# Attention: two heads share one product with V, 256 columns wide

## What is computed

```python
rep = N_HEADS // N_KV_HEADS          # 2: two heads share one K and V
kk = jnp.repeat(kk, rep, axis=1)
v = jnp.repeat(v, rep, axis=1)
att = jnp.einsum('shd,thd->hst', q, kk) / np.sqrt(HEAD_DIM)
causal = jnp.tril(jnp.ones((S, S), bool))
att = jnp.where(causal[None], att, jnp.finfo(att.dtype).min)
att = jax.nn.softmax(att, axis=-1)
attn_out = jnp.einsum('hst,thd->shd', att, v).reshape(S, N_HEADS * HEAD_DIM) @ wo
```

## Time and profile before

| | us |
|---|---|
| median of 3 runs | 2893.99 (2890.41 to 2895.43) |
| profiled execution, its time | 2896.59 |
| its span, first to last instruction | 2893.9 |
| attention loop of the first half | 1214.2 to 1260.6 |
| attention loop of the second half | 2416.6 to 2488.7 |

### The profile page before, as it was taken

The page is one execution under the profiler, slowest core; times in us unless marked ns, Lnnn a source line. Parts: engine busy times, 40 slices in busy tenths (PEclk is TensorE's granted clock), DMA queues, the critical chain, the costliest instruction groups (busy, mean ns, idle before and its releaser), DMA issues. The chain is left out here.

```text
span 2893.9 us, 33670 instructions
## 1 busy us (share of the span) xinstructions
PE 2383.4 (82%) x11480; PEld 1635.3 (57%) x11480; DVE 2070.8 (72%) x2611; ACT 1636.1 (57%) x3494; POOL 1621.8 (56%) x728
## 2 busy tenths in 40 slices
PE   8967887777788549896887888887886799999998
PEld 3345555555555318554666766665553485578863
DVE  5669999999999766425999999998997654210000
ACT  4578878888887343335887777886772313210000
POOL 0079999999999310005998998998993100000000
PEclk9979999999999759998999999998998899999999
DMA  7722242432522497742335325335225852244443
GB/s 275 264 77 81 81 144 73 137 108 66 167 66 62 165 372 285 255 174 100 99 95 179 102 92 179 101 93 178 92 76 206 306 181 66 84 142 153 153 153 102
DMA packets 236953, 418.47 MB, mean 145 GB/s; under 512 B 33904, under 2 KB 117872, under 8 KB 233968
## 3 DMA queue, kind: packets, MB, share of 16 engines
q1 hardware_dynamic: 223280, 360.22, 38.5%
q10 hardware_dynamic: 12160, 51.39, 4.5%
q0 software_dynamic: 1344, 4.72, 0.4%
HBM read 332.38 MB, written 83.89 MB: 144 GB/s over the span
## 5 line engine op out<-in xcount | busy, mean ns | idle before, releaser
L640 POOL TENSOR_TENSOR s_x<-s_du,k_bB 128x2048 f32<-128x2048 f32 (+1 forms) x256 | 881.5, 3456 | 30.9 <-issue 18.7
L716 PE MATMUL s_py<-k_ident,s_x 128*128 128x128 f32 x4096 | 562.1, 282 | 188.8 <-DVE s_x L1021 115.9
L716 PEld LDWEIGHTS s_py<-k_ident,s_x 128*128 128x128 f32 x4096 | 478.5, 145 | 410.2 <-DVE s_x L1021 192.7
L967 ACT ACTIVATE s_pA<-s_delta,k_negA 128x512 f32<-128x512 f32 x768 | 500.3, 681 | 184.4 <-DVE s_x L1021 179.3
L647 POOL TENSOR_TENSOR s_x<-s_hp,k_bC 128x1024 f32<-128x1024 f32 x192 | 452.4, 2371 | 28.0 <-DVE s_hp L1040 27.9
L1708 PE MATMUL l_p<-l_hT,l_ring 128*128 128x256 f32 x1792 | 389.6, 380 | 2.3 <-DVE l_hT L1899 1.3
L1021 DVE TENSOR_TENSOR s_x<-s_pA,k_bC 128x1024 f32<-128x1024 f32 x320 | 383.8, 1199 | 7.2 <-DMA k_bC<-scratch_xd 7.1
L1708 PEld LDWEIGHTS l_p<-l_hT,l_ring 128*128 128x128 f32 x1792 | 341.8, 191 | 50.0 <-issue 1.9
L867 ACT ACTIVATE s_xT<-s_duT,k_BT 128x128 f32<-128x128 f32 x1024 | 335.9, 387 | 0.1
L1040 DVE TENSOR_TENSOR_SCAN s_pA<-s_pA,s_x 128x512 f32<-128x512 f32 x256 | 302.5, 1215 | 39.9 <-ACT s_pA L967 39.3
L1040 DVE TENSOR_TENSOR_SCAN s_pA<-s_pA,s_carry,s_x 128x512 f32<-128x512 f32 x256 | 316.1, 1266 | 0.8 <-ACT s_pA L967 0.5
(11 more groups left out here) (212 smaller groups left out, 3669.1 us busy)
## 6 DMA issues: line engine op xcount, KB each, us to landing
k_bC<-scratch_xd SPq DMA_DIRECT2D x32, 1024.0 KB, 10.1
scratch_ug<-p_ug ACTq DMA_DIRECT2D x16, 1024.0 KB, 4.3
k_u<-scratch_ug SPq DMA_DIRECT2D x64, 256.0 KB, 3.5
k_bB<-scratch_xd SPq DMA_DIRECT2D x16, 1024.0 KB, 9.8
s_gy<-scratch_ug SPq DMA_DIRECT2D x64, 256.0 KB, 4.4
s_xt<-in_x SPq DMA_DIRECT2D x64, 256.0 KB, 4.7
scratch_x<-s_xt SPq DMA_DIRECT2D x64, 256.0 KB, 2.3
r_x<-scratch_x SPq DMA_DIRECT2D x32, 512.0 KB, 9.4
```

Of the source, the lines that this page charges most:

```text
L640: pool.tensor_tensor(out=x[:, 4 * g:4 * g + many], in0=du[:, s % 2:s % 2 + 1].broadcast_to([P, many, HALF]), in1=bB[:, 3 * g + g % 2:3 * g ...
L716: last = nc.tensor.matmul(py[:, a], x[:, n, a * P:(a + 1) * P], ident[:], is_transpose=True, start=False, stop=is_last and a == HALF // P - 1)
L967: nc.scalar.activation(out, delta[:, s % 2], ACT.Exp, scale=negA[:, s % NE, n:n + 1]).then_inc(dA_ready, 1)
```

## The change

The order of the combinations becomes: head = n // 4 * 2 + n % 2 and batch = n // 2 % 2. The two heads that share K and V come one after the other for the same batch, so the tile counts go 1, 1, 2, 2 in the first half and 3, 3, 4, 4 in the second. `probT` holds the pair side by side for each tile, twice its size before. PE makes one product with V for a pair, of 256 columns instead of 128, in every second step only (c - 3 odd), when the second of the pair is ready. ACT copies the outputs of both heads in one instruction of 256 columns. The other operations stay as they are, in the new order. ACT's copy to `probT` now writes blocks of 128 with a gap of 128 between them.

```diff
+    def head_of(n):
+        return n // (2 * SPAN) * 2 + n % 2
+    def batch_of(n):
+        return n // 2 % SPAN
+    def keys_of(n):
+        return (first + batch_of(n) + 1) * P
-    probT = sb("probT", [P, 2, KEYS * P])
+    probT = sb("probT", [P, 2, KEYS, 2, P])
...
-                if 0 <= c - 3 < COMBOS:
-                    n, kv = c - 3, (c - 3) // SPAN * NKV // NH
-                    tiles = first + n % SPAN + 1
+                if 0 <= c - 3 < COMBOS and (c - 3) % 2:
+                    n, m, kv = c - 3, (c - 3) // 2, head_of(c - 3) * NKV // NH
+                    tiles = keys_of(n) // P
                     pe.wait_ge(probT_ready, n + 1)
-                    at_least(pe, o_ready, n - 1)
+                    at_least(pe, o_ready, m - 1)
                     for b in range(tiles):
-                        last = nc.tensor.matmul(side[2 + n % 2][:, 0:P], v[:, b, kv * DH:(kv + 1) * DH],
-                                                probT[:, n % 2, b * P:(b + 1) * P], start=b == 0, stop=b == tiles - 1)
+                        last = nc.tensor.matmul(side[2 + m % 2][:, 0:2 * P], v[:, b, kv * DH:(kv + 1) * DH],
+                                                probT[:, m % 2, b].rearrange("p j s -> p (j s)"), start=b == 0, stop=b == tiles - 1)
...
                     act.wait_ge(p_turned, n + 1)
-                    at_least(act, o_done, n - 1)
-                    nc.scalar.activation(probT[:, n % 2, 0:end], side[n % 2][:, 0:end], ACT.Copy).then_inc(probT_ready, 1)
+                    at_least(act, o_done, m - 1)
+                    nc.scalar.activation(probT[:, m % 2, 0:tiles, n % 2], side[n % 2][:, 0:tiles * P].rearrange("p (b s) -> p b s", s=P),
+                                         ACT.Copy).then_inc(probT_ready, 1)
...
-                    nc.scalar.activation(o[:, head, a * P:(a + 1) * P], side[2 + n % 2][:, 0:P], ACT.Identity,
-                                         bias=cols[:, bv:bv + 1]).then_inc(o_ready, 1)
+                    nc.scalar.activation(o[:, head:head + 2, a * P:(a + 1) * P], side[2 + m % 2][:, 0:2 * P].rearrange("p (j s) -> p j s", s=P),
+                                         ACT.Identity, bias=cols[:, bv:bv + 1]).then_inc(o_ready, 1)
```

More of the change, by code:

```diff
@@ L1744, in _ @@
                 if c < COMBOS:
-                    n, head, a = c, c // SPAN, c % SPAN
-                    end = (first + a + 1) * P
+                    n, head, a, end = c, head_of(c), batch_of(c), keys_of(c)
                     at_least(pe, expd, n - 3)
@@ L1755, in _ @@
                     at_least(pe, probT_ready, n - 1)
-                    for b in range(first + n % SPAN + 1):
+                    for b in range(keys_of(n) // P):
                         last = nc.tensor.transpose(side[n % 2][:, b * P:(b + 1) * P], prob[:, n % 4, b * P:(b + 1) * P], ident[:])
                     last.then_inc(p_turned, 1)
-                if 0 <= c - 3 < COMBOS:
-                    n, kv = c - 3, (c - 3) // SPAN * NKV // NH
-                    tiles = first + n % SPAN + 1
+                if 0 <= c - 3 < COMBOS and (c - 3) % 2:
+                    n, m, kv = c - 3, (c - 3) // 2, head_of(c - 3) * NKV // NH
+                    tiles = keys_of(n) // P
                     pe.wait_ge(probT_ready, n + 1)
-                    at_least(pe, o_ready, n - 1)
+                    at_least(pe, o_ready, m - 1)
                     for b in range(tiles):
-                        last = nc.tensor.matmul(side[2 + n % 2][:, 0:P], v[:, b, kv * DH:(kv + 1) * DH],
-                                                probT[:, n % 2, b * P:(b + 1) * P], start=b == 0, stop=b == tiles - 1)
+                        last = nc.tensor.matmul(side[2 + m % 2][:, 0:2 * P], v[:, b, kv * DH:(kv + 1) * DH],
+                                                probT[:, m % 2, b].rearrange("p j s -> p (j s)"), start=b == 0, stop=b == tiles - 1)
                     last.then_inc(o_done, 1)
@@ L1770, in _ @@
             for k in range(NH):
-                pe.wait_ge(o_ready, SPAN * (k + 1))
+                pe.wait_ge(o_ready, SPAN * (k // 2 + 1))
                 rows_of(T_WO + k, o[:, k], acc, k == 0, k == NH - 1).then_inc(w_used, 1)
@@ L1842, in _ @@
                 if c < COMBOS:
-                    n, j, end = c, c % 4, (first + c % SPAN + 1) * P
+                    n, j, end = c, c % 4, keys_of(c)
                     act.wait_ge(biased, n + 1)
@@ L1848, in _ @@
                 if 0 <= c - 2 < COMBOS:
-                    n, end = c - 2, (first + c % SPAN + 1) * P
+                    n, m, tiles = c - 2, (c - 2) // 2, keys_of(c - 2) // P
                     act.wait_ge(p_turned, n + 1)
-                    at_least(act, o_done, n - 1)
-                    nc.scalar.activation(probT[:, n % 2, 0:end], side[n % 2][:, 0:end], ACT.Copy).then_inc(probT_ready, 1)
-                if 0 <= c - 3 < COMBOS:
-                    n, head, a = c - 3, (c - 3) // SPAN, (c - 3) % SPAN
+                    at_least(act, o_done, m - 1)
+                    nc.scalar.activation(probT[:, m % 2, 0:tiles, n % 2], side[n % 2][:, 0:tiles * P].rearrange("p (b s) -> p b s", s=P),
+                                         ACT.Copy).then_inc(probT_ready, 1)
+                if 0 <= c - 3 < COMBOS and (c - 3) % 2:
+                    m, head, a = (c - 3) // 2, head_of(c - 4), batch_of(c - 3)
                     bv = QK + head * NKV // NH
-                    act.wait_ge(o_done, n + 1)
-                    if n == 0 and not last_half:
+                    act.wait_ge(o_done, m + 1)
+                    if m == 0 and not last_half:
                         for j in range(LATE):
                             act.wait_ge(late_out[j], 16 * len(range(j, SPAN * NE, LATE)))
-                    nc.scalar.activation(o[:, head, a * P:(a + 1) * P], side[2 + n % 2][:, 0:P], ACT.Identity,
-                                         bias=cols[:, bv:bv + 1]).then_inc(o_ready, 1)
+                    nc.scalar.activation(o[:, head:head + 2, a * P:(a + 1) * P], side[2 + m % 2][:, 0:2 * P].rearrange("p (j s) -> p j s", s=P),
+                                         ACT.Identity, bias=cols[:, bv:bv + 1]).then_inc(o_ready, 1)
             for b in range(SPAN):
@@ L1973, in _ @@
                 if c < COMBOS:
-                    n, j, end = c, slice(c % 4, c % 4 + 1), (first + c % SPAN + 1) * P
+                    n, j, end = c, slice(c % 4, c % 4 + 1), keys_of(c)
                     dve.wait_ge(scores, n + 1)
@@ L1980, in _ @@
                 if c:
-                    n, j, end = c - 1, slice((c - 1) % 4, (c - 1) % 4 + 1), (first + (c - 1) % SPAN + 1) * P
+                    n, j, end = c - 1, slice((c - 1) % 4, (c - 1) % 4 + 1), keys_of(c - 1)
                     dve.wait_ge(expd, n + 1)
```

## The result

The changed kernel takes 2895.95 us in the median of 20 runs, the kernel before 2890.55 us in 20 runs beside them. The ratio is 1.002, with a 95% interval of 1.0012 to 1.0028: 5.4 us slower, 0.2%, somewhere between 3.5 and 8.1 us. The forecast was +4.9 us. As a time it was 2898.9 us, 3 us above what was measured: it was added to the 2893.99 us of the first three runs of the kernel before, and 20 runs of the same kernel have their median at 2890.55. The profiled execution has a span of 2896.6 us.

A forecast was written before the change was run, and what follows sets the result against it. It took a closed chain of softmax latency, one product with V and one set of scores as the bound. Second half +5.7 and first half -0.8 gave +4.9 us, a median of 2898.9 us, range 2892.5 to 2904.5.

The forecast's parts named there:

- the chain: Attention loops: a turn is one softmax latency, one product with V and one set of scores; 4.40 and 2.83 us before.
- Link A: Second half, working on 4 tiles and waiting for the copy of 3: 4.49 us from mask to next odd-step mask.
- link B: Second half, working on 3 tiles and waiting for the copy of 4: 5.00 us to the next odd-step mask.
- first half's turn: First attention loop, four steps from mask to mask: 5.52 us against 5.66 before.
- Exit: Last mask of a loop to first product with wo: second half 6.96 us (+1.1), first half 4.2 (+0.3).
- The sum: Both attention loops together: second half +5.7 us, first half -0.8, in all +4.9 us.
- rival 1: ACT's gapped copy to probT costs extra per block: slower, up to +12.6 us in all; chance 12%.
- Rival 2: PE is the bound and the wide product's columns are free: faster, -12 us net, 2882 us; chance 8%.
- Rival 3: The loops' ends are covered, say by transfers, or other effects cancel: no change, 2894 to 2896 us; chance 7%.
- Rival 4: PE's clock falls because of its pauses: slower, over +50 us with the second loop at half clock; chance 3%.

The follow-up runs named there:

- e4: Kernel before plus one extra 0.22 us product, unused by any output, ahead of the product with V in each even combination; ratio 0.9996 to the kernel before.
- e5: Kernel before plus one extra 0.22 us product, unused by any output, ahead of the product with V in each odd combination; ratio 1.0023 to the kernel before.
- e7: Changed kernel with the pair's product as two groups of 128 columns at the same place; ratio 1.0023 to the kernel before.
- e2: Changed kernel with the pair's product with V and its output copy one step later; ratio 0.9979 to the kernel before.
- e8: Kernel before with its single 128 column product one step later and ahead of the transpositions; ratio 0.9948 to the kernel before.

## Why the prediction was right

**The mechanism.** The statement on which it turned, that of the two products with V in a turn only one is in the chain, is shown by e4 and e5; that the burst behind the wait costs and not its width, by e7. This and the turns are what the prediction is right by. That its total comes within 0.5 us of the measured one is in part luck: the interval of the measured difference is 4.6 us wide.

**The turn.** Link A was reckoned 4.49 and measured 4.48; link B 5.00 and 4.99; first half's turn 5.52 and 5.51. The tie that I saw in link A (transpositions done at 2.38, copy at 2.43) is there: the product's weight load starts 2.43 us behind the mask and PEld is idle for only 0.18 us ahead of it. The chain view takes the other side of the tie, the transpositions, in link A; the prediction's sentence that all of the pair's product stands behind the copy to probT is thus quite true of link B only.

**Exit.** The last rows of PE in the second half's loop, then the first product with wo (this answers to the earlier trace rows):

```profile
2487.78 0.60 PE L1765 MATMUL l_p<-l_ident,l_work 128*128 128x128 f32 x4
2489.07 1.99 PE L1773 MATMUL l_p<-l_probT,l_v 128*128 128x256 f32 x8 [0.69 <-ACT l_probT L1860]
2490.90 1.45 PE L1724 MATMUL l_p<-l_ring,t_hidden 128*128 128x512 f32 x3
```

The last mask is at 2483.94, so the exit is 6.96 us, as reckoned (6.96, before 5.82). In the first half it is 4.25 (reckoned 4.2).

**The sum.** Second half +5.6 (forecast +5.7), first half -0.9 (-0.8). The kernels differ by 5.4 us in their medians, 4.7 in the two loops.

**What hid what.** ACT's output copy, the gapped copy to probT and the fewer instructions cost nothing, as argued: 0.473 us off the chain; 0.588 and 0.480 for four and three blocks against 0.589 and 0.482 dense. So rival 1 falls. Rival 2 falls by the product: 1.83 us for 8 instructions with a first load is 0.215 each. By the Trainium skill's gap figures ("TensorE: Matmul & The Clock Gate", Back-to-back issue gap) the pair would have been cheaper than two singles, and for this float32 product the trace does not agree: 0.215 us against 0.111. Rival 3, that the loops' ends are covered, does not show: in the eight experiments the loops change by between +7.1 and -16.5 us, and the times of the kernels follow them within 1.2 us. One profile could not tell, since the stretch between the two loops varies from 1147.6 to 1157.2 us in the ten of them. Rival 4: PE pauses in each turn and the granted clock stays 1.00.

**What it left out.** The prediction counted the new order as part of the sum and never asked what it brings alone. It reckoned the change as one step from 8.80 to 9.49; the runs show two, from 8.80 to 8.34 by the order and from there to 9.47 by the pairing. And the theory of one chain was too simple for the repair: e2 missed by 7 us, since I had followed only the wait that was removed and not what is queued behind the next wait in PE's order.

## What to carry to other kernels

In a pipeline over engines, write down the closed chain of one turn, and ask of each piece of work whether it stands in it: merging two short operations into one long one can move the one that was under cover into the chain. Issue a long operation whose inputs are old ahead of the short one that still has to wait; a delay of one step takes a wait away, but only the place in the queue decides what stands behind the next one. And if a change is made of two (here order and width), reckon each alone: one half of this was worth 9.5 us, and the other cost 14.

## What the runs showed of the hardware

- A float32 product with V that must wait takes 0.10 to 0.11 us more than one that need not: 1.83 us to the next scores against 1.73 for 8 instructions of 256 columns (the changed kernel, e2), 1.00 against 0.89 for 8 of 128 (the kernel before, e8). I take this for the first weight load: in e2 it starts 0.11 us ahead of its product (2432.73 and 2432.84), in the changed kernel the two start together (2433.90). Behind it come 0.216 us for each instruction of 256 columns and 0.111 for each of 128; a wide one is thus only a few ns cheaper than two narrow ones.
- A busy share of PE of 97 to 98% went with 0% to 100% of added work being hidden: in the kernel before the view showed PE 43.24 of 44 us busy in the middle of the loop, and ten products of 0.22 us still found room there. Durations of matrix instructions overlap (0.27 us for 0.11 of streaming), and short waits vanish in them; PEld's idle time shows them.
- ACT's writing with gaps of 128 elements between blocks of 128 cost nothing that the rows can show: 0.588 us for four blocks against 0.589 dense, 0.480 for three against 0.482.
